# Attention row maxima: the diagonal piece starts from the full piece's maximum, and the merge step goes

## What is computed

```python
q = proj(w_q, b_q)
k = proj(w_k, b_k)
v = proj(w_v, b_v)
scores = jnp.einsum('bhqd,bhkd->bhqk', q, k) / np.sqrt(D_K).astype(np.float32)
causal = jnp.tril(jnp.ones((S, S), dtype=bool))
scores = jnp.where(causal, scores, -jnp.inf)
attn = jax.nn.softmax(scores, axis=-1)
out = jnp.einsum('bhqk,bhkd->bqhd', attn, v).reshape(B, S, D_MODEL)
```

## Time and profile before

| | |
|---|---|
| median of 3 runs | 3025.01 us |
| lowest, highest | 3016.74, 3033.07 us |
| span of the profiled execution | 3027.5 us |
| granted TensorE clock over the span | 0.985 |
| busy, share of the span: PE, DVE, POOL, ACT | 96%, 72%, 61%, 44% |
| attention stage | some 606 to 1646 us of the span |

### The profile page before, as it was taken

One profiled execution on the slowest core, in us unless ns is written; L12 is line 12 of the kernel. 1 busy time (PEld: TensorE's weight loads), 2 busy tenths in 40 slices (PEclk: granted clock), 3 DMA queues, 4 the chain that ended last, 5 costly groups with the idle time before them and its releaser, 6 DMA issues.

```text
span 3027.5 us, 49806 instructions
## 1 busy us (share of the span) xinstructions
PE 2895.4 (96%) x16480; PEld 2168.3 (72%) x16480; DVE 2179.3 (72%) x5344; ACT 1341.6 (44%) x2436; POOL 1833.5 (61%) x1077
## 2 busy tenths in 40 slices
PE   8999999999999999999999989999999999989997
PEld 5788888766666666666666677777777787767775
DVE  6555555678787878787877687777777787756664
ACT  2222222156666666666666522233222333226664
POOL 1233222278888888888886256766565666655664
PEclk9999999999999999999999999999999999999998
DMA  7655555756655665566555333332322322238996
GB/s 240 211 187 201 187 180 180 233 114 136 137 124 115 138 138 121 115 139 140 119 117 160 107 97 93 94 112 74 103 79 93 102 85 81 73 107 222 239 245 118
DMA packets 281948, 420.53 MB, mean 139 GB/s; under 512 B 48463, under 2 KB 132687, under 8 KB 281742
## 3 DMA queue, kind: packets, MB, share of 16 engines
q1 hardware_dynamic: 259214, 384.22, 44.9%
q0 software_dynamic: 22528, 33.72, 5.8%
HBM read 263.38 MB, written 153.01 MB: 138 GB/s over the span
## 4 chain that ended last, share of the span: by engine, by line
PE 53%; DVE 14%; POOL 14%; issue 8%; ACT 4%; DMA 4%; another core or an unknown queue 2%; DVEq 1%; POOLq 0%; SPq 0%; ACTq 0%
PE qkv_ps_m L840 12%; PE ffn_ps_m L2191 11%; POOL att_gathered L1105 6%; PE qkv_ps_m L844 6%; POOL att_pt L1098 5%; PE att_ps_o L1330 5%; PE att_ps_p L1386 4%; PE att_ps_s L1304 4%; DMA out<-exp_y,exp_tok_add 2%; PE exp_ps_u L1607 2%; PE exp_ps_y L1623 1%; PE att_ps_s L1361 1%; DVE ffn_att L147 1%; DVE ffn_x L149 1%
## 5 line engine op out<-in xcount | busy, mean ns | idle before, releaser
L247 DVE CUSTOM_DVE_ANT_0 att_ps_s<-att_ps_s,att_causal 128x512 f32<-128x512 f32 (+1 forms) x992 | 469.3, 502 | 175.5 <-PE att_ps_s L1304 171.3
L1166 ACT ACTIVATE att_pt<-att_ps_p 128x512 f32<-128x512 f32 (+1 forms) x1024 | 524.5, 589 | 143.6 <-PE att_ps_p L1389 110.2
L1304 PE MATMUL att_ps_s<-att_ks,att_qs 96*128 96x512 f32 x1488 | 513.4, 373 | 2.2 <-DVE att_lower L253 0.6
L1386 PE MATMUL att_ps_p<-att_qs,att_ks 98*128 98x512 f32 (+3 forms) x1536 | 498.5, 364 | 9.3 <-ACT att_pt L1166 8.0
L1098 POOL TENSOR_TENSOR att_pt<-att_pt 128x1024 f32<-128x1024 f32 (+2 forms) x153 | 331.1, 2164 | 166.6 <-PE att_ps_o L1330 144.8
L1105 POOL TENSOR_TENSOR att_gathered<-att_gathered,att_pt 128x2048 f32<-128x2048 f32 (+1 forms) x92 | 388.1, 4218 | 7.2
L1912 POOL DMA_INDIRECT slot_info<-ffn_info,ffn_slot x256 | 275.9, 1078 | 119.3 <-issue 76.5
L253 DVE TENSOR_REDUCE att_lower<-att_ps_s 128x1 f32<-128x512 f32 x496 | 339.2, 684 | 7.4 <-PE att_ps_s L1304 7.4
L1386 PEld LDWEIGHTS att_ps_p<-att_qs,att_ks 98*128 98x128 f32 x1536 | 272.6, 191 | 82.1 <-issue 34.7
L1304 PEld LDWEIGHTS att_ps_s<-att_ks,att_qs 96*128 96x128 f32 x1488 | 275.7, 191 | 73.3 <-DVE att_rowmax L247 27.7
L577 POOL TENSOR_TENSOR qkv_x<-qkv_x,qkv_mod 128x512 f32<-128x512 f32 x60 | 83.4, 1391 | 371.5 <-DVE qkv_x L671 371.5
(11 more groups left out here) (311 smaller groups left out, 6718.8 us busy)
## 6 DMA issues: line engine op xcount, KB each, us to landing
att_qs<-qk_parts SPq DMA_DIRECT2D x96, 512.0 KB, 6.8
att_ks<-qk_parts SPq DMA_DIRECT2D x96, 512.0 KB, 12.7
qk_parts<-qkv_out_hi SPq DMA_DIRECT2D x128, 256.0 KB, 2.2
qk_parts<-qkv_out_lo SPq DMA_DIRECT2D x128, 256.0 KB, 2.4
qkv_x<-x SPq DMA_DIRECT2D x16, 1024.0 KB, 5.6
v_rows<-qkv_out_v SPq DMA_DIRECT2D x64, 256.0 KB, 2.3
att_vs<-v_rows SPq DMA_DIRECT2D x32, 512.0 KB, 16.1
o_parts<-att_o SPq DMA_DIRECT2D x64, 256.0 KB, 7.9
```

The costliest lines, as they stand in the source:

```text
L247: dve.tensor_tensor_reduce(part, part, self.causal[:, UNIT - (c1 - c0):UNIT], scale=1.0, scalar=MASKED, op0=ALU.add, op1=ALU.max, accum_ou ...
L1166: act.activation(tile(c)[:, h, col:UNIT], ps_p[(NPROB * prev.g + n) % NP][:, col:UNIT], ACT.Exp, scale=float(HD) ** -0.5).then_inc(exp_don ...
L1304: pe.matmul(bank("s", cur.g, i)[:, 0:c1 - c0], qs[cur.slot][0:STACK, h, t * P:(t + 1) * P], ks[cur.slot][0:STACK, h, c0:c1], start=True, s ...
L1386: last = pe.matmul(part[:, i * (UNIT - col):(i + 1) * (UNIT - col)], ks[prev.slot][:, h + i, kt * P:(kt + 1) * P], qs[prev.slot][:, h + i, ...
```

## The change

The order of the pieces becomes full, small, diagonal. The diagonal piece's `tensor_tensor_reduce` takes the column of `lower` that the full piece two places earlier wrote as its first value (a scalar operand read from SBUF, one value per partition) in place of the constant, and waits for that piece's signal on `max_done`. The merge, its wait and its signal go, so `NMAX` is `N1`.

```diff
@@ -80,10 +80,10 @@
-ORDER = [(h, t) for a in range(KT // 2) for h in range(GH) for t in (KT - 1 - a, a)]
-PIECES = [(h, t, c0, min(c0 + UNIT, (t + 1) * P)) for h, t in ORDER for c0 in range(0, (t + 1) * P, UNIT)]
+PIECES = [piece for a in range(KT // 2) for h in range(GH)
+          for piece in ((h, KT - 1 - a, 0, UNIT), (h, a, 0, (a + 1) * P), (h, KT - 1 - a, UNIT, (KT - a) * P))]
 N1 = len(PIECES)
-NMAX = N1 + 1
+NMAX = N1
@@ -244,8 +244,13 @@
         if c1 == (t + 1) * P:
             dve.wait_ge(self.s_done, CREDIT + N1 * g + i + 1)
             dve.sem_inc(self.mark, 1)
+            below = MASKED
+            if c0:
+                low = h * LOW + t - LOW
+                below = under[:, low:low + 1]
+                dve.wait_ge(self.max_done, CREDIT + NMAX * g + i - 1)
             dve.tensor_tensor_reduce(part, part, self.causal[:, UNIT - (c1 - c0):UNIT], scale=1.0,
-                                     scalar=MASKED, op0=ALU.add, op1=ALU.max,
+                                     scalar=below, op0=ALU.add, op1=ALU.max,
                                      accum_out=rows[:, h * KT + t:h * KT + t + 1]).then_inc(self.max_done, 1)
@@ -254,11 +259,6 @@
     def negate(self, dve, g, bank):
 
-        rows, under = self.rowmax[g % 2], self.lower[g % 2]
-        dve.wait_ge(self.max_done, CREDIT + NMAX * g + N1)
-        dve.sem_inc(self.mark, 1)
-        upper = rows[:, :].rearrange("p (h t) -> p h t", t=KT)[:, :, LOW:KT]
-        dve.tensor_tensor(upper, upper, under[:, :].rearrange("p (h t) -> p h t", t=LOW), ALU.max).then_inc(self.max_done, 1)
         dve.wait_ge(self.mt_done, CREDIT + g + 1)
```

## The result

| | before | changed |
|---|---|---|
| median, us | 3017.99 (20 runs) | 3029.65 (20 runs) |
| lowest, highest, us | 2999.56, 3033.07 | 3015.14, 3041.12 |
| span of the profiled execution, us | 3027.5 | 3030.1 |

The ratio is 1.0043, with a 95% interval of 1.0028 to 1.0057: slower by 0.4%, which is inside the 0.5% that the prediction counted as no change, and for the most part clear of zero. With more runs the median of before has come down from 3025 to 3018, so the change costs some 12 us on the medians (13 by the ratio, 8 to 17 by its interval).

A forecast was written before the change was run, and what follows sets the result against it. PE's program sets the pace, DVE counting only where PE waits for it. Stretch 1 +0.24, stretch 2 +0.15, turn -0.09: +0.30 us in each of 31 periods, +9 us, 3034 on the median; range 3015 to 3060.

The forecast's parts named there:

- stretch 1: Pieces 13 to 28, where DVE works through: 4 scalars +0.24, narrower piece 13 -0.06, wider piece 28 +0.06; sum +0.24 us.
- stretch 2: Pieces 29 to 47: DVE 0.27 later, wide small piece where PE waits, less 0.12 from narrower piece 47; sum +0.15 us.
- The merge: DVE's 2.39 us merge before the turn, 72 us in all: removed, but DVE has nothing else to do there.
- The rival in which they count: DVE's freed 72 us count before the turn: 27 us come back, 2998 or about 3007 us; chance 0.06.
- a gain of 0.09 us a group from the turn: Turn after the totals block: 0.97 after its start instead of 1.06 once the merge goes, 0.09 us a group.
- 0.06 us for the scalar: Each of 16 diagonal pieces: SBUF scalar adds 0.06 us, from 751 against 691 ns in another instruction; bounds 0 to 0.12.
- the sign that the prediction named: In the changed profile, diagonal pieces about 0.06 us longer than small ones of equal width.
- Pieces 0 to 12: With pieces 29 to 35 they carry 6 more scalars; no bank wait of PE found there, so zero.
- The weigh blocks: Attention group: weigh block of c = 4 0.24 us later, that of c = 8 0.4 us later.
- The wait on the full piece: Diagonal piece's wait: the signal is 0.11 us old when its turn comes, so it costs nothing.
- Groups: Attention stage: groups at 33.8 us in place of 33.5.
- POOL did not hold up the scalar's instruction: Rival at the 16 diagonal pieces: scalar read waits for POOL up to 2.39 us each, some 700 us more; chance 0.02.

The follow-up runs named there:

- no_merge: Kernel before with the merge removed and diagonal pieces starting from the constant 450 (old order, no SBUF scalar): group 33.46 us, ratio 1.0009.
- scalar_only: Kernel before with the new order, merge kept, diagonal pieces reading a mask column from SBUF without waiting for the full piece: group 33.67 us, ratio 1.0027.
- old_order_seed: Changed kernel without its new order: diagonal piece directly behind its full piece, taking its maximum and waiting for its signal, no merge: group 34.84 us, ratio 1.0132.
- order_only: Kernel before with the new order of pieces, old constant and merge kept: group 33.55 us, ratio 1.0006.

## Why the prediction came out right

**The forecast.** 3034 was forecast and 3029.65 measured, and no change in the sense of 0.5% was the likeliest case and came. As a difference the forecast was +9 us on the median it had, and some +12 came. That the two are close is partly luck. The groups give 5.6 us where the sum gave 9.3, and the rest is not in the sum; and the median it started from, 3025 of 3 runs, has come down to 3018 with 20, from which the same sum would have given 3027. Within a group the sum said 0.30 us and 0.19 came, because its errors partly cancel: 0.18 too much in stretch 1 and 0.05 too much in stretch 2, against a gain at the turn that did not come and a cost ahead of the weigh block of c = 0 that was put at nothing.

**The merge** was read right where it mattered: its 2.39 us on DVE, 72 us in all, were worth nothing, and DVE's idle time before L266 has taken their place. The rival in which they count is excluded by no_merge. The turn comes 0.97 after the totals block, as forecast.

**The step that failed first: a gain of 0.09 us a group from the turn.** The step ended at the turn itself and did not ask what is late next. The next wait, for ACT, starts from the totals and not from the turn; 0.03 us remain in the old order. In the new order nothing remains, since there the merge would not have delayed the turn at all (scalar_only).

**The step that failed second: 0.06 us for the scalar.** The term was mis-sized; it measured 0.022. The instructions of the earlier trace rows do differ by 0.06, and where the scalar's instruction stands right behind a full piece, as in old_order_seed, the price is 0.07. Even the sign that the prediction named held: diagonal pieces are 0.05 to 0.07 longer in the changed profile than small ones of equal width, 601 against 555 ns for 384 and 356 against 286 for 128:

```profile
L252 DVE CUSTOM_DVE_ANT_0 att_ps_s<-att_ps_s,att_causal,att_lower 128x384 f32<-128x384 f32 x108 | 65.0, 601 | 0.1
L252 DVE CUSTOM_DVE_ANT_0 att_ps_s<-att_ps_s,att_causal 128x384 f32<-128x384 f32 x106 | 58.9, 555 | 0.0
...
L252 DVE CUSTOM_DVE_ANT_0 att_ps_s<-att_ps_s,att_causal,att_lower 128x128 f32<-128x128 f32 x105 | 37.3, 356 | 0.0
L252 DVE CUSTOM_DVE_ANT_0 att_ps_s<-att_ps_s,att_causal 128x128 f32<-128x128 f32 x108 | 30.9, 286 | 0.0
```

But the length of an instruction is not what it adds to a queue. 0.043 of that difference is paid by a second `tensor_tensor_reduce` in a row, scalar or none, and before the change the small piece paid it.

**Stretch 1** was to cost 0.24 and costs 0.06 (9.83 to 9.90 in the table above, 0.062 before rounding). From DVE's start (1017.41, now 1017.30) to PE's piece 28 (1023.52, now 1023.49) it took 6.11 and takes 6.19: +0.08, which is 4 scalars at 0.022. The two smaller terms came too: DVE starts 0.09 sooner after the weigh block of c = 0 (0.06 forecast), and the wider piece 28 puts off the next weigh block by 0.06, as forecast. The working by places was right, with the wrong price in it.

**Stretch 2** was to cost 0.15 and costs 0.10. Its largest part, the wide small piece where PE waits, was seen rightly: 0.05 of it is there in order_only, without any scalar.

**Pieces 0 to 12** were put at nothing. Against no_merge, which has the same early turn, the changed kernel is 0.05 us longer there. PE's loads do wait there: for DVE's banks 0.03 us a group before and 0.09 in the changed kernel, and for ACT, ahead of the problems, 0.22 and 0.43 (means). Which of the two makes the 0.05 is not shown.

**The weigh blocks** of c = 4 and c = 8 were forecast 0.24 and 0.4 us later in the group. Counted from the turn they are 0.18 and 0.28 later (medians), and 0.07 of each is only that the turn itself is earlier, as in no_merge.

**The wait on the full piece** was priced at nothing, and the runs bear that out to 0.04 us a group at most, and to 0.01 beside the scalar; behind its full piece directly it would have cost 0.12 a piece.

**Groups** were forecast at 33.8 and are 33.67. POOL did not hold up the scalar's instruction (the longest of the 512 diagonal pieces took 0.76 us), as the prediction had argued from L733.

**What no step had**: anything outside the groups. The prediction took the clock of before as given for the changed kernel. In single executions the first turn of the stage moved by 6 us, which is as much as the groups' terms together.

## What to carry to other kernels

Take a step off an engine's queue only after asking who waits at its end, and then who is waited for next: 72 us of DVE time were worth 0.03 us a group. Price an added operand by the distance between starts of neighbouring instructions at the place where it will stand, not by the lengths of two instructions elsewhere. Parts of a change do not simply add: what the merge's removal gained in the old order was gone in the new one. And when a result of two pieces ahead costs 0.02 us a time while one of the piece just ahead costs 0.19 (0.12 of later start and 0.07 of scalar), order the work so that producer and consumer have something between them.

## What the runs showed of the hardware

- A `tensor_tensor_reduce` right behind another holds DVE 0.043 us longer than the same behind a TENSOR_REDUCE (0.248 and 0.206 for 128 columns, 0.515 and 0.473 for 384; start to start).
- A first value read from SBUF, one per partition, adds 0.022 us behind another `tensor_tensor_reduce`, 0.07 behind a TENSOR_REDUCE whose end it had to wait for, and 0.06 after idle time (0.54 from start to accumulator read in old_order_seed, 0.48 before).
- A wait of DVE on its own signal costs nothing on DVE if the producer is two pieces back (1.46 us for three pieces with and without it). Where it waits for the instruction just ahead, and takes its result as scalar, it starts 0.12 us later (0.72 after it in place of 0.60).
- The granted clock fell to 0.50 for 13.7 to 17.1 us at the start of the attention stage in 7 of 14 profiled executions, with PE all but fully busy in it, and cost some 5 to 6 us. It began 3.5 to 5.1 us after the stage's first score matmul, behind waits of PE of 0.54 and 0.2 us that the other 7 have too. It went with a difference of half a microsecond in PE's standing some 10 us earlier (less standing, more often the low clock); the cause is open.
